# Two attentions over a rounded image: the image as its own keys, the matrix on queries and results, both in one stage of 32 tasks

## The reference, cut to what matters

```
def bitnet_linear(x, W, b):                        # W: [out, in], entries of qW are -1, 0, 1
    w_scale = jnp.maximum(jnp.mean(jnp.abs(W)), 1e-05)
    qW = jnp.sign(W) * (jnp.abs(W) > 0.5 * w_scale).astype(W.dtype)
    i_scale = jnp.maximum(jnp.max(jnp.abs(x)), 1e-08) / 127.0
    qx = jnp.clip(jnp.round(x / i_scale), -128.0, 127.0)
    return jnp.einsum('...i,oi->...o', qx, qW) * (w_scale * i_scale) + b
...
vis = bitnet_linear(dinov2_features, W_d2v, b_d2v)
image_embeds = bitnet_linear(vis, W_img, b_img)    # 32 x 1500 x 128
fused = bitnet_linear(text_embeddings, W_txt, b_txt)   # 32 x 56 x 128
for Wa, ba in ((W_att0, b_att0), (W_att1, b_att1)):    # W: [64, 128]
    kv = bitnet_linear(image_embeds, Wa, ba)
    k = jnp.concatenate([kv, kv], axis=-1)
    scores = jnp.einsum('bse,bpe->bsp', fused, k) * inv_sqrt_e
    attn = jax.nn.softmax(scores, axis=-1)
    fused = fused + 0.1 * jnp.einsum('bsp,bpe->bse', attn, k)
```

## Time and profile before

| | us |
|---|---|
| median of 3 runs | 5559.77 (5553.78 to 5563.06) |
| the profiled execution | 5560.35 |
| its span | 5558.8 |
| TensorE busy in the span | 4114.8 (74%) |
| VectorE | 2733.2 (49%) |
| ScalarE | 2195.4 (39%) |
| GpSimd | 1146.3 (21%) |
| the two calls of `bit_attend` | 257.7 and 256.1 |
| mean granted TensorE clock | 0.845 of 2.4 GHz |

### The profile page before, as it was taken

How to read it: one execution, slowest core, us unless ns; L and a number is a source line. 1 busy time by engine, 2 the same in 40 slices (tenths; PEclk the granted TensorE clock), 3 DMA queues, 4 the chain that set the end, 5 groups by cost and what they waited for, 6 DMA issues and landing times. The chain is left out here.

```text
span 5558.8 us, 88140 instructions
## 1 busy us (share of the span) xinstructions
PE 4114.8 (74%) x33170; PEld 2636.3 (47%) x33170; DVE 2733.2 (49%) x2907; ACT 2195.4 (39%) x2705; POOL 1146.3 (21%) x1410
## 2 busy tenths in 40 slices
PE   6388888717389999799996422277758688787885
PEld 6256666504246666466663100154533255555553
DVE  6522222333244432344432476654543588888993
ACT  5256666401023333132331258632321265555652
POOL 0111111030323222232320000000000455454520
PEclk8689999859589999799997755598978699998997
DMA  4155555316122221122210130000000355555540
GB/s 119 52 123 123 124 119 116 83 54 215 33 65 65 70 64 42 49 72 63 70 52 13 50 91 0 1 0 1 0 0 13 82 124 129 121 130 117 132 101 14
DMA packets 143213, 401.83 MB, mean 72 GB/s; under 512 B 31987, under 2 KB 45471, under 8 KB 142874
## 3 DMA queue, kind: packets, MB, share of 16 engines
q1 hardware_dynamic: 111778, 352.71, 25.1%
q0 software_dynamic: 26624, 44.18, 3.6%
q10 hardware_dynamic: 4608, 2.10, 0.1%
HBM read 238.53 MB, written 8.09 MB: 44 GB/s over the span
## 5 line engine op out<-in xcount | busy, mean ns | idle before, releaser
L1816 DVE TENSOR_REDUCE L_mp<-ps 112x2 f32<-112x1000 f32 x384 | 458.3, 1199 | 700.6 <-PE ps L1700 700.6
L1801 ACT ACTIVATE L_p<-ps 125x896 f32<-125x896 f32 x384 | 352.2, 917 | 875.1 <-PE ps L1725 802.9
L1737 PE MATMUL ps<-L_p,L_cn 125*97 125x448 f32 x1536 | 639.2, 538 | 0.0
L2452 DVE TENSOR_REDUCE L_mp<-ps 112x2 f32<-112x1000 f32 x384 | 456.9, 1194 | 131.9 <-PE ps L2253 120.3
L2417 ACT ACTIVATE L_p<-L_p 125x896 f32<-125x896 f32 x384 | 364.7, 950 | 263.0 <-DVE L_p L2469 262.9
L2469 DVE SCALAR_TENSOR_TENSOR L_p<-ps,L_lb 125x896 f32<-125x896 f32 x384 | 414.9, 1081 | 21.5 <-DMA L_lb<-L_low 11.0
L879 ACT ACTIVATE L_p<-ps,rk 125x896 f32<-125x896 f32 x384 | 385.0, 1008 | 80.9 <-PE ps L761 78.6
L1723 PE MATMUL ps<-L_qh,L_ch 97*125 97x448 f32 x768 | 401.1, 522 | 14.3 <-DMA L_qh<-L_mc 14.3
L1737 PEld LDWEIGHTS ps<-L_p,L_cn 125*97 125x97 f32 x1536 | 250.4, 163 | 205.7 <-issue 165.9
L2285 PE MATMUL ps<-L_p,L_vs 125*32 125x112 f32 x6144 | 241.0, 277 | 119.3 <-ACT L_p L2417 92.5
L2253 PE MATMUL ps<-L_ks,L_qs 96*128 96x500 bf16 x768 | 251.0, 414 | 71.6 <-DMA L_ks<-L_k_part 42.7
(11 more groups left out here) (473 smaller groups left out, 7416.0 us busy)
## 6 DMA issues: line engine op xcount, KB each, us to landing
L_ks<-L_k_part SPq DMA_DIRECT2D x288, 375.0 KB, 7.6
L_ks<-L_k_first SPq DMA_DIRECT2D x96, 375.0 KB, 5.7
moe_w<-in_L_w SPq DMA_DIRECT2D x64, 512.0 KB
L_cn<-in_ctxN SPq DMA_DIRECT2D x32, 568.4 KB
cs_ct<-in_ctxT SPq DMA_DIRECT2D x32, 562.5 KB, 4.3
L_ct<-in_ctxT SPq DMA_DIRECT2D x32, 562.5 KB, 4.5
L_raw<-in_ctxT SPq DMA_DIRECT2D x32, 562.5 KB
L_cr<-in_ctxT POOLq DMA_DIRECT2D x32, 562.5 KB, 4.9
```

The costliest lines, as they stand in the source:

```text
L1737: mm = nc.tensor.matmul(U[:, a, :], CN[s][:, j, :], P[:, n % 2, a * HALF:(a + 1) * HALF], start=(j == 0), stop=(j == KT - 1))
L1801: nc.scalar.activation(two(P[:, n % 2, :]), SB[n % 2], ACT.Exp).then_inc(S["exped"].sem, 1)
L1816: nc.vector.tensor_reduce(mp[:, 2 * k:2 * k + 2], ps[0:TT, bank:bank + 2, 0:500], AX.X, ALU.max).then_inc(S["chunk_maxed"].sem, 1)
L2452: nc.vector.tensor_reduce(mp[:, 2 * c:2 * c + 2], ps[0:TT, CB[pair], 0:500], AX.X, ALU.max).then_inc(S["chunk_maxed"], 1)
```

## The change

The keys are no longer made. The rounded image itself is the keys and the values, and the matrix is applied to the 56 queries of an image before the scores and to the 56 results after the weighing. Both attentions become one block with 32 tasks (attention, pair). Their order (`attend_order`) is three tasks of attention 0, then attention 1 and 0 in turn: (0,0), (0,1), (0,2), (1,0), (0,3), (1,1), (0,4) and so on to (1,15). Each task has an image pair; (1,i) needs the `FU` that (0,i) left.

For each task:

- `query`: TensorE multiplies the pair's 112 query columns by the matrix (f32), ScalarE copies them to `QW`.
- `parts`: GpSimd splits `QW` into three bf16 parts (a copy, a subtraction, a copy, a subtraction; each waits for the one before).
- `scores`: three column blocks by three parts by two images, 18 bf16 matmuls of 500 columns, each on 64 of the array's columns; the three parts add up in PSUM.
- Maximum, exponential, turning and weighing as before; the scale of the keys goes into the exponential's scale.
- `values`: the image's key rows are now the transposes of n: twelve bf16 transposes of one image, in two groups (8 and 4) by ScalarE to `VT` (f32, four buffers). There is one image for each of the first 28 tasks and four images ahead of them, so each image is turned once, not once per attention.
- `turn_out` as before; then ScalarE copies the result (`copy_out`), TensorE applies the matrix (`project`, f32, 112 columns), ScalarE makes 0.1·(c·result + b) (`make_add`) and GpSimd adds it to `FU` (`fuse`).

Gone are `keys`, `keys_by_row`, their two copies, the load of the bias rows (`brow`) and the hardware loops: all tasks are written out. PSUM banks: 0 to 2 scores, 3 and 4 turned `P` (4 also the first values), 5 weighed, 6 the last values, 7 queries and results.

```
-            for which in ("att0", "att1"):
-                bit_attend(core, bit, Vb, FU[:, 0, :], which)
+            bit_attend(core, bit, Vb, FU[:, 0, :])
...
+                def query(j):
+                    a, i = order[j]
+                    if j >= 1:
+                        pe.wait_ge(S["q_copied"], j)
+                    if j >= 3:
+                        pe.wait_ge(S["add_made"], j - 2)
+                    if a == 1:
+                        pe.wait_ge(S["fused"], place[0, i] + 1)
+                    nc.tensor.matmul(ps[:, 7, 0:2 * NQ], WT[:, a, :], columns(i), start=True,
+                                     stop=True).then_inc(S["q_made"], 1)
...
+                def scores(j):
+                    i = order[j][1]
+                    pe.wait_ge(S["parts_ready"], j + 1)
+                    if j >= 1:
+                        pe.wait_ge(S["exped"], j)
+                    for c in range(3):
+                        for m in range(3):
+                            for s in range(2):
+                                lo = (2 * i + s) * NK + c * 500
+                                mm = nc.tensor.matmul(ps[64 * s:64 * s + 64, c, 0:500], FB[j % 2][:, m, s, :],
+                                                      V[:, lo:lo + 500], start=(m == 0), stop=(m == 2))
+                    mm.then_inc(S["scored"], 1)
...
+                for j in range(NJ):
+                    turn(j, 0)
+                    turn(j, 1)
+                    if j + 1 < NJ:
+                        scores(j + 1)
+                    turn(j, 2)
+                    if j >= 1:
+                        turn_out(j - 1)
+                    b = j + AHEAD
+                    if b < B:
+                        pe.wait_ge(S["pt_copied"], 3 * j + 2)
+                        values_first(b)
+                    if j >= 1:
+                        project(j - 1)
+                    if b < B:
+                        values_last(b)
+                    weigh(j)
+                    if j + 2 < NJ:
+                        query(j + 2)
...
+                    nc.scalar.activation(VT[k % 4][:, b % 2, lo:hi, :].rearrange("p t n -> p (t n)"),
+                                         ps[0:KP, bank, :].bitcast(BF16)[:, 0:(hi - lo) * 128],
+                                         ACT.Copy).then_inc(S["vt_copied"], 1)
...
+                def parts(j):
+                    f = FB[j % 2]
+                    pool.wait_ge(S["q_copied"], j + 1)
+                    if j >= 2:
+                        pool.wait_ge(S["scored"], j - 1)
+                    nc.gpsimd.tensor_copy(f[:, 0, :, 0:NQ], QW[:, :, :]).then_inc(S["hi_made"], 1)
+                    pool.wait_ge(S["hi_made"], j + 1)
+                    nc.gpsimd.tensor_tensor(rest[:, :, :], QW[:, :, :], f[:, 0, :, 0:NQ],
+                                            ALU.subtract).then_inc(S["hi_off"], 1)
+                    pool.wait_ge(S["hi_off"], j + 1)
+                    nc.gpsimd.tensor_copy(f[:, 1, :, 0:NQ], rest[:, :, :]).then_inc(S["mid_made"], 1)
+                    pool.wait_ge(S["mid_made"], j + 1)
+                    nc.gpsimd.tensor_tensor(f[:, 2, :, 0:NQ], rest[:, :, :], f[:, 1, :, 0:NQ],
+                                            ALU.subtract).then_inc(S["parts_ready"], 1)
```

More of the change, by code:

```diff
@@ L3414, in _ @@
                             mm.then_inc(S["lifted"], 1)
-def bit_attend(core, bit, V, FU, which):
-    nc, d, ps = core.nc, core.d, core.ps
[L3422 to L3426, removed]
-    with ExitStack() as ctx:
[L3428 to L3447, removed]
-        with nc.Block() as block:
[L3450 to L3453, removed]
@@ L3455, in _ @@
             @block.gpsimd
             def _(pool):
[L3457 to L3463, removed]
@@ L3530, in _ @@
-            @block.scalar
-            def _(act):
-                act.sem_inc(S["exped"], 1)
-                def copy_keys(i, s):
-                    act.wait_ge(S["k_made"], 2 * i + s + 1)
-                    nc.scalar.activation(KTs[:, s, :].rearrange("p (a m) -> p a m", a=3),
-                                         ps[:, 3:6, 0:500], ACT.Identity, scale=sc,
-                                         bias=v(core, which)).then_inc(S["kt_copied"], 1)
-                def body(i, p, nxt):
-                    if nxt:
-                        copy_keys(i + 1, 0)
-                    act.wait_ge(S["maxed"], i + 1)
-                    nc.scalar.activation(P[:, :].rearrange("p (a m) -> p a m", a=3), ps[:, 0:3, 0:500],
-                                         ACT.Exp, bias=sm[:, 0:1], scale=float(D) ** -0.5,
-                                         accum_out=sm[:, 1:2]).then_inc(S["exped"], 1)
-                    if nxt:
-                        copy_keys(i + 1, 1)
-                for s in range(2):
-                    copy_keys(0, s)
-                all_pairs(act, body)
@@ new lines, in _ @@
+                for p in range(2):
+                    nc.gpsimd.memset(FB[p][:, :, :, :], 0.0).then_inc(S["padded"], 1)
+                pool.wait_ge(S["padded"], 2)
+                def parts(j):
[12 more added lines that the diff above has]
+                                            ALU.subtract).then_inc(S["parts_ready"], 1)
@@ new lines, in fuse @@
+                def fuse(j):
+                    i = order[j][1]
+                    pool.wait_ge(S["add_made"], j + 1)
+                    nc.gpsimd.tensor_tensor(columns(i), columns(i), add[:, :], ALU.add
+                                            ).then_inc(S["fused"], 1)
+                parts(0)
+                parts(1)
+                for j in range(NJ):
+                    if j >= 1:
+                        fuse(j - 1)
+                    if j + 2 < NJ:
+                        parts(j + 2)
@@ L3603, in quantized @@
+                fuse(NJ - 1)
 def quantized(core, bit, link, dst, src, k, tmp, p=128):
```

310 lines of the change are left out of this document (211 added, 99 removed).

## The result

| | before | after |
|---|---|---|
| median of the runs on the same chip | 5556.77 us (5552.94 to 5563.06, 4 runs) | 5335.97 us (5322.63 to 5342.77, 4 runs) |
| after divided by before | | 0.9602, 95% interval 0.959 to 0.9615 |
| span of the profiled execution | 5558.8 us | 5340.1 us |
| the attention stage in it | 513.8 us | 302.8 us |
| start to start, one pair or task | 15.3 us | 9.07 us |

The change is faster by 4.0%, and by 34 us more than predicted. The predicted range began at 5342 us, 6 us above the median: it missed (the slowest of the four runs, 5342.77 us, lies just inside).

A forecast was written before the change was run, and what follows sets the result against it. TensorE's queue was taken as the bound: 7.48 us a task, 8.05 at clock 0.93, plus 1.4 wait makes 9.45. Times 32, with start, end and 2%, the stage is 322 us, the whole 5370 us; range 5342 to 5425 us.

The forecast's parts named there:

- The clock: Attention stage: granted clock taken as 0.93, so TensorE's 7.48 us a task become 8.05 us.
- a clock of 0.97 to 0.90: Attention stage: the clock's spread in the forecast's own range, worth -11 to +8 us.
- projection and query: TensorE, each task: two f32 matmuls of 112 columns at 0.20 us each, 0.40 us.
- TensorE's work: Each task: turning, weighing, image transposes, turning the result, query, projection and scores sum to 7.48 us.
- wait for GpSimd: TensorE before each block of scores: stands 1.4 us for the query's copy and GpSimd's four operations.
- The 2% for seams: Attention stage: 6 us added, mainly for changes between full-array and half-array matmuls in new places.
- Serial scores: Rival, scores: two images one after the other in bf16, 66 us more, 5436 us; chance 0.08.
- GpSimd at twice its rows: Rival, GpSimd's query parts: four operations take twice 1.40 us, 45 us more, 5415 us; chance 0.10.
- the weight loads in the open: Rival, scores: weight loads not hidden, at most 39 us more, 5409 us; chance 0.05.
- parts in time: Rival, before scores: GpSimd's parts ready, 1.4 us less at the most, down to 5325 us; chance 0.04.
- A lower clock: Rival, attention stage: mean clock 0.8, 42 us more, 5412 us; chance 0.08.
- The rival on the other side: All TensorE work of the stage at the lower clock level throughout: 5586 us, slower; chance 0.01.

The follow-up runs named there:

- e9: Kernel before the change, with six unread bf16 matmuls put into TensorE's 1.77 us wait for ScalarE's key copy: 5529.73 us (kernel before: 5548.39).
- e3: Changed kernel with GpSimd's last subtraction repeated once, twice or four times, each on a wait for the one before: 5347.50, 5381.41 and 5459.53 us.
- e6: Changed kernel with each transpose of the image issued twice on TensorE: 5349.89 us (kernel before: 5553.50).
- e1: Changed kernel with one bf16 query part from GpSimd in place of three, same 18 score matmuls: 5304.75 us (kernel before: 5540.30).
- e8: Changed kernel with the images' score matmuls grouped apart and both written to one half of the array: 5397.69 us (kernel before: 5548.39).
- e7: Changed kernel with the query of task j+2 in the middle of the weighing, its ScalarE copy ahead of the exponential: 5318.65 us, 0.9575 of the kernel before.
- e3_chain_4: Changed kernel with GpSimd's last subtraction repeated four times, each on a wait: 5459.53 us, stage 441.2 us.
- e5: Kernel before the change, with key matmuls and key copies left out for all pairs but each call's first: 5571.21 us (kernel before: 5553.50).
- e10: e5 with ten unread bf16 matmuls put into TensorE's longest wait, behind keys_by_row: 5468.26 us (kernel before: 5548.39).

## Why the prediction was wrong by 34 us, with the right bound and the wrong clock

The forecast's own sum was a stage of 322 us; it took 302.8. Those 19 us are the part that the working answers for. The other 15 us are that the rest of the span came out 7.7 us shorter in the profiled execution, that the median lies 5.7 us below that execution, and rounding.

**The step that failed is "The clock".** The mean of the old stage, 0.93, was carried over to the new one: "7.48 us become 8.05 us". The inside of the new stage ran at 1.00. The old clock belonged to the old waits: 1.77 us in the middle of a pair, with 0.93 and 0.78 us soon after. e9 shows it: with that one wait filled down to 0.50 us the same kernel runs at 1.00 inside its first call, and over 130 us of its second. e3 shows when it would have been otherwise in the new order: waits of 1.10 and 1.57 us a task leave it at 1.00, 2.05 us costs a slow task in seven, 2.99 us brings 0.75. The range had "a clock of 0.97 to 0.90", so even its better end was below the truth.

With full clock and nothing else altered the forecast would have been 18 us lower, 5352 us, and the range with it: from 5324 us, which holds the measured 5335.97. The median fell out of the stated range by 6 us only, less than the 15 us that lie outside the stage's working, so that it fell out and not just in is in part chance.

**The errors by term, for a task at full clock:**

| term | forecast | measured, start to start |
|---|---|---|
| scores | 1.92 | 2.02 |
| twelve transposes of the exponential | 1.44 | 0.54 + 1.05 = 1.59 |
| turning the result | 0.20 | 0.10 |
| twelve transposes of the image | 0.75 | 0.53 + 0.32 = 0.85 |
| projection and query | 0.40 | 0.32 + 0.31 = 0.63 |
| weighing | 2.77 | 2.77 |
| TensorE's work | 7.48 | 7.96 |
| wait for GpSimd | 1.40 | 1.10 |
| a task | 8.88 | 9.06 |
| with its clock (0.93; 1.00) | 9.45 | 9.06 |

- TensorE's work was 0.48 us too small. The f32 matmuls of 112 columns cost 0.31 and 0.32 us each, not 0.20. Their columns are not the reason, or only a small part of it. The trace of before has sixteen such matmuls in a row, in another stage, that take 3.59 us to the start of the next line (0.22 us each):

```profile
1714.76 3.82 PE L1708 MATMUL ps<-L_un,L_N 96*128 96x112 f32 x32
1718.35 0.45 PE L1723 MATMUL ps<-L_qh,L_ch 97*125 97x448 f32 x1
```

  In a task each stands alone between matmuls of other forms, which fits the other 0.1 us but was not tried. The rest of the 0.48 us is 0.1 us here and there where full-array and half-array work meet; no run tried such a change alone. The 2% for seams was put there for this, 6 us, and what was missing was 0.48 us times 32, 15 us.
- The wait was 0.30 us too large: the way to and from GpSimd 0.12 us in place of 0.20, its four operations with their waits 1.58 us in place of 1.65, and the eight transposes in front 1.05 us in place of 0.96; the rest is that 1.35 us was rounded up to 1.4. Its mechanism, releaser and place were as forecast, and so were the prices scaled from the earlier trace rows: 0.28 and 0.40 us.
- With 0.48 more and 0.30 less, a task at full clock was forecast 0.18 us too short, 6 us over 32 tasks. The clock added 0.57 us that did not come, 18 us, and the 2% 6 us more: 18 us too long together, with a seam of 1 us at the ends. The range allowed both, but each only in part.

**Right, and shown:** TensorE's order sets the end (e6: more work there costs its length; e1: less wait gains its length); the halves run side by side in bf16 (e8); the weight loads are hidden; the start takes 14 us; the exponential is ready before TensorE asks. That ScalarE is nearly on the path came out in e7, where its exponential, pushed back by the query's copy, held TensorE for 0.11 us a task.

**The rivals.** Serial scores fell by e8, GpSimd at twice its rows by the timeline (its four operations take 1.58 us), the weight loads in the open by the loads beside the scores (below), and parts in time by the wait of 1.10 us. "A lower clock" did not happen, but e3_chain_4 shows that its mechanism is real and larger than priced: its tasks take 13.65 us where 7.96 of work and 2.99 of wait make 10.95, so 2.7 us times 32, 86 us, go to the clock, where 42 us were named. The rival on the other side, the low level, seems nearer than its 0.01: e5 is a variant of the old kernel that is slower although work was taken out, and e10 gets the time back with fillers alone. By e3 the new order is about 1 us of wait away from the first slow tasks and nearly 2 from every task being slow.

## What to carry to other kernels

Don't carry a stage's mean clock over to a stage with other waits. List the waits of a period in the old and in the new order. Where the new ones are shorter, the longest and all together (here 1.10 us against 1.77, 0.93 and 0.78), forecast with full clock as the likely case and keep the old clock for the range. When an edit takes work from TensorE but leaves it waiting for another engine, look at the granted clock before counting the gain: e5 lost all of it. And price a small matmul that stands alone from one that stands alone: in a row of sixteen it took 0.22 us, alone between other forms 0.31.

## What the runs showed of the hardware that was not expected

- **Clock and waits.** In the new order's loop, one wait of 1.10 or 1.57 us a task left the granted clock at 1.00 inside the stage; 2.05 us gave 0.98, with the lower level every seventh task; 2.99 us gave 0.75. In the old order, 2.77 us with a wait of 0.78 us behind it (e5) gave 0.73 over the stage. Ten unread matmuls in a wait made a kernel 103 us faster (e5 to e10, one run each, on two chips; 85.7 us of it in the stage's windows).
- **Halves of the array.** Eighteen bf16 matmuls of 500 columns took 2.09 us over two halves and 3.98 us on one, and 2.10 us where three matmuls of one half stood in a row in the queue.
- **Weight loads.** The loads of the scores by the source view of their line (ns least, median, most; first and last start):

```profile
L3486 PEld LDWEIGHTS ps<-bit_V,bat_fb x576: 106/110/178, 3588.2 to 3871.7; 128*64 128x64 bf16 x192
```

  Eighteen of 110 ns are 1.98 us of loading in a block that takes 2.09 us with its matmuls: all of it lies beside them, though the rows are the same in all. The Trainium skill (TensorE: Matmul & The Clock Gate, Part 3, The mechanism) lets a load overlap matmuls in flight only where the row group differs; this trace does not agree. (The same section also lets a load go ahead into a background weight buffer; the trace does not show which way these loads took.) Even on one half, in e8, 18 matmuls with 18 loads take 3.98 us, 0.22 each, against 0.213 for the key matmuls of before.
- **ScalarE and bf16.** Reading bf16 out of PSUM went at f32's pace: 1.02 us for 1024 columns, 0.60 us for 512, as taken.
